# A message-passing kernel: grid of 36 slots instead of 32, five PSUM banks for its groups, and the block's maximum in PSUM

## What is computed

```python
z = x @ enc_node_w + enc_node_b           # of relu(layernorm(x))
e = edge_attr @ enc_edge_w + enc_edge_b
def genconv(z, e, src, dst, w1, b1, g1, bb1, w2, b2, t):
    msg = relu(z[src] + e) + 1e-7
    m = msg * t
    ex = exp(m - segment_max(m, dst)[dst])
    agg = segment_sum(msg * ex, dst) / segment_sum(ex, dst)
    out = z + agg
    return relu(layernorm(out @ w1 + b1) * g1 + bb1) @ w2 + b2
# layer 0: h = genconv(z, ...); layers 1..3: h += genconv(relu(layernorm(h)), ...)
# result: x + relu(layernorm(h))
```

## Time and profile before

| | us |
|---|---|
| median of 3 runs (6206.5 to 6214.1) | 6207.28 |
| the profiled execution, its own time | 6218.0 |
| its span, first to last instruction | 6213.7 |
| `prepare`, 0 to 509 | 509 |
| `lay`, 509 to 1759.5 | 1250.5 |
| layers 0, 1, 2 (to 2860, 3965, 5071) | 1100.5, 1105, 1106 |
| the last layer, 5071 to 6213.7 | 1142.7 |

### The profile page before, as it was taken

How to read it: one execution, slowest core, us unless ns; L and a number is a source line. 1 busy time by engine, 2 the same in 40 slices (tenths; PEclk the granted TensorE clock), 3 DMA queues, 4 the chain that set the end, 5 groups by cost and what they waited for, 6 DMA issues and landing times. The chain is left out here.

```text
span 6213.7 us, 106997 instructions
## 1 busy us (share of the span) xinstructions
PE 4575.7 (74%) x43556; PEld 3238.2 (52%) x43557; DVE 4593.2 (74%) x7210; ACT 2450.6 (39%) x3848; POOL 4185.6 (67%) x3850
## 2 busy tenths in 40 slices
PE   7715888999938777783777877468777756777786
PEld 6715777888825444452445544244544533454443
DVE  9431555444438999994899999489999957888887
ACT  2403566654513444441444443234434423333333
POOL 3054777766547777774777777377777747777775
PEclk8955888666669998896899889789988978898888
DMA  8971777665564555544455555445555534454552
GB/s 344 417 239 66 260 275 282 221 234 221 194 192 167 180 174 185 177 164 118 157 178 183 175 176 177 126 144 179 170 183 177 184 130 136 165 173 165 169 173 88
DMA packets 323285, 1168.13 MB, mean 188 GB/s; under 512 B 142130, under 2 KB 145380, under 8 KB 255444
## 3 DMA queue, kind: packets, MB, share of 16 engines
q1 hardware_dynamic: 172852, 890.91, 38.7%
q0 software_dynamic: 134800, 214.63, 13.7%
q10 hardware_dynamic: 15120, 55.50, 2.2%
HBM read 910.82 MB, written 249.92 MB: 187 GB/s over the span
## 5 line engine op out<-in xcount | busy, mean ns | idle before, releaser
L1258 POOL DMA_INDIRECT gb<-ztab,ovi x2704 | 2945.6, 1089 | 1025.3 <-issue 833.6
L1356 PE MATMUL bank<-ep_mid,keep 128*128 128x512 f32 (+3 forms) x3474 | 1568.1, 610 | 18.8 <-DVE ep_mid L1346 18.8
L1356 PEld LDWEIGHTS bank<-ep_mid,keep 128*128 128x128 f32 x3474 | 699.3, 203 | 853.1 <-issue 820.7
L1309 DVE TENSOR_REDUCE mx<-xb 128x64 f32<-128x2816 f32 (+17 forms) x196 | 1016.7, 5187 | 3.6
L1273 PE MATMUL bank<-zpw,oh_layers 128*128 128x64 bf16 x28812 | 879.7, 194 | 155.9 <-DMA zpw<-ztab 155.9
L1273 PEld LDWEIGHTS bank<-zpw,oh_layers 128*128 128x128 bf16 x28812 | 874.3, 98 | 211.1 <-DMA zpw<-ztab 156.9
L1096 POOL DMA_INDIRECT ecell<-zpw,ptg x588 | 646.8, 1100 | 228.1 <-issue 176.7
L1404 PE MATMUL bank<-keep,na 128*128 128x128 f32 x100 | 47.5, 475 | 952.8 <-DVE na L1401 952.8
L925 PE MATMUL bank<-byk,zpw 88*88 88x102 f32 (+13 forms) x4608 | 665.1, 332 | 53.0 <-DVE zpw L906 49.1
L925 PEld LDWEIGHTS bank<-byk,zpw 88*88 88x88 f32 (+13 forms) x4608 | 654.5, 234 | 62.8 <-DVE zpw L906 54.0
L1319 ACT ACTIVATE cm<-top_x,nt 128x64 f32<-128x64 f32 x196 | 68.2, 348 | 1501.4 <-DVE top_x L1313 1484.9
(11 more groups left out here) (222 smaller groups left out, 5784.6 us busy)
## 6 DMA issues: line engine op xcount, KB each, us to landing
oh_layers<-ohd SPq DMA_DIRECT2D x196, 1568.0 KB, 9.8
ea_in<-in_ea SPq DMA_DIRECT2D x101, 512.0 KB, 8.1
enc<-es_out ACTq DMA_DIRECT2D x101, 512.0 KB
cb<-rowc SPq DMA_DIRECT2D x49, 1024.0 KB
gb<-ztab,ovi POOLq DMA_INDIRECT x2704
ohd<-oh_lay SPq DMA_DIRECT2D x49, 576.0 KB
xb<-ecell SPq DMA_DIRECT2D x20, 1408.0 KB
ohd<-oh_lay SPq DMA_DIRECT2D x49, 512.0 KB
```

What stands on the lines that cost most here:

```text
L1258: at["g"][d] = ga_l[d % 2](GP.indirect_dma_start(gb[d % 2][:, 64 * v:64 * v + 64], None, T["ztab"], bass.IndirectOffsetOnAxis(ap=ovi[:, i: ...
L1309: q = V(VE.tensor_reduce(mx[:, 0:64], x_of(d, 0, S.S[d]).rearrange("p (s f) -> p f s", f=64), AX.X, ALU.max))
L1356: q = PE.matmul(both[d % 2][:, 0:w], ident, rows[:, 128 * (c - a):128 * (c - a) + w], start=(c == 0), stop=(c + 4 >= S.S[d]), skip_group_c ...
```

## The change

G becomes 36, with 23 groups of one source block and 13 of two. `OVER` becomes 36, 21, 20, ... 5, 628 in all, so that V is 5, 36, 6, 21, 6, 20, 7, ... 12 and the slots are 49*36 + 628 = 2392. A block's grid has five groups of eight (the last of four), each with its bank: `gps` is banks 0 to 4. `both` is one bank, 5; `NA` and `NB` are the halves of bank 6; `top_x` is 128 columns of bank 7. ScalarE makes `cm` from `mx`, now two tiles by turns, with a Relu of its own ahead of the exponential. The two bias products move behind TensorE's wait for ScalarE. The sums of block d wait for the fold of block d-1. In `lay`, `pick` takes 6 slots at a time in place of 20.

```diff
-OVER = (39, 23, 21, 20, 19, 19, 18, 18, 17, 17, 17, 16, 16, 16, 16, 15, 15, 15, 15, 14, 14, 14, 14,
+OVER = (36, 21, 20, 19, 18, 18, 17, 17, 16, 16, 16, 15, 15, 15, 15, 14, 14, 14, 14, 13, 13, 13, 13,
...
-        self.singles = 15
+        self.singles = 23
...
-            hit = sb("hit", [128, 20 * KS], FP32, yc)
+            hit = sb("hit", [128, 6 * KS], FP32, yc)
-                for a in range(0, S.S[d], 20):
-                    n = min(20, S.S[d] - a)
+                for a in range(0, S.S[d], 6):
+                    n = min(6, S.S[d] - a)
-                share = 1.1 * (len(eights) * (len(units[u]) + put) + 4 * put + 1) / steps
+                share = 1.1 * (len(eights) * (len(units[u]) + put) + 9 * put + 1) / steps
...
-                n_gp = 4
+                n_gp = 5
-                gps = bank[0:4]
-                both, NA, NB = bank[4:6], bank[6], bank[7]
+                gps = bank[0:5]
+                both, NA, NB = bank[5], bank[6][:, 0:256], bank[6][:, 256:512]
+                top_x = bank[7][:, 0:128].rearrange("p (a f) -> p a f", a=2)
...
+                    top = mx[:, 64 * (d % 2):64 * (d % 2) + 64]
-                    q = V(VE.tensor_reduce(mx[:, 0:64], x_of(d, 0, S.S[d]).rearrange(
+                    q = V(VE.tensor_reduce(top, x_of(d, 0, S.S[d]).rearrange(
-                    q = k["topx"][d] = V(VE.tensor_scalar(top_x[:, d % 2, :], mx[:, 0:64], 0.0,
+                    q = k["topx"][d] = V(VE.tensor_scalar(top_x[:, d % 2, :], top, 0.0,
-                    q = A(AE.activation(cm[:, u % 2, i, :], top_x[:, d % 2, :], ACT.Exp,
+                    q = A(AE.activation(cm[:, u % 2, i, :], top, ACT.Relu))
+                    AE.wait_ge(ae_s, q)
+                    q = A(AE.activation(cm[:, u % 2, i, :], cm[:, u % 2, i, :], ACT.Exp,
...
-                    if i == 0 and d >= 2:
-                        PE.wait_ge(ve_s, k["fold"][d - 2])
+                    if i == 0 and d:
+                        PE.wait_ge(ve_s, k["fold"][d - 1])
...
                     q = A(AE.copy(ot[:, :], NB[:, 0:128]))
-                    PE.matmul(NA[:, 0:256], ident, b1, start=True, stop=False)
                     yield
                     PE.wait_ge(ae_s, q)
+                    PE.matmul(NA[:, 0:256], ident, b1, start=True, stop=False)
                     q = P(PE.matmul(NA[:, 0:256], ot[:, :], w1, start=False, stop=True))
...
-                    PE.matmul(NA[:, 0:128], ident, b2, start=True, stop=False,
-                              skip_group_check=True)
                     yield "turned"
...
                     PE.wait_ge(ae_s, q)
+                    PE.matmul(NA[:, 0:128], ident, b2, start=True, stop=False,
+                              skip_group_check=True)
```

More of the change, by code:

```diff
@@ L19 @@
 RSQRT_SEED = 0x5F3759DF
-OVER = (39, 23, 21, 20, 19, 19, 18, 18, 17, 17, 17, 16, 16, 16, 16, 15, 15, 15, 15, 14, 14, 14, 14,
-        13, 13, 13, 13, 12, 12, 12, 12, 12, 11, 11, 11, 11, 10, 10, 10, 10, 9, 9, 9, 9, 8, 8, 7, 7, 6)
+OVER = (36, 21, 20, 19, 18, 18, 17, 17, 16, 16, 16, 15, 15, 15, 15, 14, 14, 14, 14, 13, 13, 13, 13,
+        12, 12, 12, 12, 12, 11, 11, 11, 11, 11, 10, 10, 10, 10, 9, 9, 9, 9, 8, 8, 8, 7, 7, 6, 6, 5)
 EDGES = (64,) + (54,) * 2 + (52,) * 2 + (50,) * 4 + (48,) * 8 + (46,) * 8 + (44,) * 10 + (42,) * 14
@@ L57, in __init__ @@
         self.ones = [sum(n for _, n in self.groups[:s]) for s in range(self.G + 1)]
-        assert self.ones[-1] == self.ND and self.G == 32
+        assert self.ones[-1] == self.ND and self.G == 36
         self.sorted = [d // 2 if d % 2 else self.ND - 1 - d // 2 for d in range(self.ND)]
@@ L93 @@
 for _n, _w in (("ident", 128), ("iota", 128), ("be", 128), ("prow", 2),
-               ("base", 32), ("full", 49), ("iota1", 128), ("we", 128), ("wn", 128), ("bn", 128), ("cen", 128),
+               ("base", 36), ("full", 49), ("iota1", 128), ("we", 128), ("wn", 128), ("bn", 128), ("cen", 128),
                ("ms", 2), ("lower", 128), ("shift", 128), ("wrap", 128), ("node", 49),
@@ L720, in sorted_path @@
                 mx = sb("mx", [128, 64 * -(-S.SP // 2)], FP32, fc)
-                top_x = sb("top_x", [128, 2, 64], FP32, fc)
                 cm = sb("cm", [128, 2, 2, 64], FP32, fc)
@@ L727, in sorted_path @@
                 oh2 = sb("oh_layers", [128, 2, 128 * S.ones[-1]], BF16, fc)
-                layer_args = (oh2, z, h, npd, wri, dci, outi, ovi, xb, gb, mx, top_x, cm, ds, nt,
+                layer_args = (oh2, z, h, npd, wri, dci, outi, ovi, xb, gb, mx, cm, ds, nt,
                               zb, zr)
@@ L1200, in layer @@
         def layer(number, tag, args):
-            (oh, z, h, npd, wri, dci, outi, ovi, xb, gb, mx, top_x, cm, ds, nt, zb, zr) = args
+            (oh, z, h, npd, wri, dci, outi, ovi, xb, gb, mx, cm, ds, nt, zb, zr) = args
             final = tag == "last"
@@ L1355, in mul @@
                         w = 128 * min(4, b - c)
-                        q = PE.matmul(both[d % 2][:, 0:w], ident, rows[:, 128 * (c - a):128 * (c - a) + w],
+                        q = PE.matmul(both[:, 0:w], ident, rows[:, 128 * (c - a):128 * (c - a) + w],
                                       start=(c == 0), stop=(c + 4 >= S.S[d]),
@@ L1366, in fold @@
                     k["fold"][d] = V(VE.tensor_reduce(
-                        ds[:, u % 2, i, :], both[d % 2][:, :].rearrange("p (g c) -> p c g", g=4),
+                        ds[:, u % 2, i, :], both[:, :].rearrange("p (g c) -> p c g", g=4),
                         AX.X, ALU.add))
```

## The result

The changed kernel takes 6311.68 us (median of 4 runs, 6284.73 to 6323.16), the kernel before 6210.69 on the same chip (median of 4 runs, 6206.5 to 6214.76): ratio 1.0156, 95% interval 1.0122 to 1.019. That is 101 us slower; forecast was 6350. The profiled execution took 6307.63 us, its span is 6303.2.

The account below looks back on a forecast made before the run. VectorE was taken to pace the three middle layers, GpSimd the last. Middle layers +59 each (+177), last layer -27, layout -8: total +142 us, so 6218.0 becomes 6360 profiled, median about 6350; range 6285 to 6405.

Parts of the forecast that it names:

- VectorE's added work: Per layer: more reduction, sub, mul and a fifth add, less over; together 57.4 us, about 52 with overlap, taken as 55.
- waits ahead of the splitting: Middle layers: VectorE's waits for ScalarE's casts shrink by 9 us, and by 3 more from shorter first slices.
- wait for `hb`: Every layer: only the fifth add covers this step, so VectorE waits 0.55 us 25 times, +14 us.
- L1432, now L1435: Node chain: later bias products and longer sums use up TensorE's slack, so this wait grows by 6 us a layer.
- start: Start of each layer: the first two blocks have 41 gathers in place of 45, -5 us.
- last node stage: End of each layer: the last node stage adds 1 us.
- crowded first pairs: Last layer: nearly all of 103 us of gather waits goes, but 5 us is kept for these pairs.
- (1): Splitting in middle layers: the 1.62 us wait stays for the second cast, only 0.36 goes; -9 us, and -3 from shorter exponentials.
- (2): Step waiting for `hb`: no longer covered by over, VectorE waits 0.55 us there, +14 us in every layer.
- shorter rounds of `pick`: Layout: a round no longer holds TensorE up, about 1 us for each of two rounds in seven units, -15 us.
- The rival of the wider units: Layout: four units widened to 96 to 100 columns leave the low clock, each 9 us shorter, total 6315; 25%, inside the range.
- `turn_back`: Layout: its copies grow with the slots by 6%, some 0.8 us in each of nine units, +7 us.

Follow-up runs that it names:

- experiment 7: Changed kernel with separate banks for NA and NB, bias products ahead of TensorE's wait, and the maximum in SBUF: 6264.86 us.
- experiment 6: Changed kernel without the two node-stage steps that follow the fifth add, so the old order of steps: 6283.53 us.
- experiment 2: Changed kernel with the maximum back in SBUF, everything else as changed: 6309.61 us.
- experiment 1: Kernel before with only the maximum moved to PSUM, and one bank for the sums to make room: 6167.36 us, ratio 0.9941.
- experiment 3: Changed kernel with one more node-stage step ahead of the first sub, for earlier casts: 6185.14 us.

## Why the prediction was right, and where its sizes were off

The side, the mechanism and the place were right, and the time lay in the range; the sum was 52 us too high, 23 of them in the middle layers, 20 in the last and 9 ahead of layer 0. Point by point, for the third layer:

| term of the sum | forecast | measured |
|---|---|---|
| VectorE's added work | +55 | +49.7 |
| waits ahead of the splitting | -12 | -10.9 (49.7 to 38.8) |
| wait for `hb` | +14 | +11.6 (1.7 to 13.3) |
| L1432, now L1435 | +6 | +4.9 (10.3 to 15.2) |
| start | -5 | -5.0 (36.1 to 31.1) |
| last node stage; measured at the layer's last fold | +1 | +2.4 (L1366, now L1369, 10.9 to 13.3) |
| sum | +59 | +52.7; the stretch grew by 51.2 |

Two of the waits before, which the rows ahead of the prediction don't have:

```profile
DVE ds L1366 <- PE bank L1356: 10.9, 2, 9.2
...
DVE na L1439 <- ACT hb L263: 1.7, 2, 0.8
```

**VectorE's added work** is the term that was mis-sized most. Its instructions add up to 55.7 us more (the sums by line: the fifth `add` 20.3, the reduction 16.5, `sub` 10.7, `mul` 11.8, `over` -3.3, the others together -0.3), near the 57.4 of the sum; but the engine is busy only 49.7 us longer (940.3 to 990.0), since 6.0 us lie under their neighbours. The prediction had measured this overlap, worked 52 out of it, and then took 55 without a reason. That is 5 of the 8 us by which each middle layer was over-estimated, some 16 us of the 52. The wait for `hb` gives 2 more: the sum took all of it for new.

**What each part cost.** Of the 51.2 us of the third layer, 10.3 go with the banks and the bias products undone (experiment 7), 3.3 with the moved steps (experiment 6), none with the maximum's place (experiment 2). The other 38 are left for the wider grid itself, by subtraction: no run has it alone.

**The last layer** lost 42.4 us, not 22. Its waits for gathers fell by 109.3 us (136.9 to 27.6): all but the start, so that the 5 us kept for crowded first pairs was too much. VectorE's work grew by 53.0, its wait for `hb` by 11.6 (1.7 to 13.3), and L1435 did not grow at all (13.8 to 13.4). That TensorE's longer chain shows in a middle layer and not in this one, I can't explain.

**GpSimd.** The prediction held that the gathers beside `sub` make no difference to the sum, because VectorE has no room; experiment 2 shows it for the changed kernel. It holds only there: in the kernel before the same relief is worth 41 us (experiment 1), all in the last layer. Of the gathers that start while L1332 runs, 306 of 389 take more than 1.05 us in the trace of before, in the mean 0.54 us more than one alone, and beside L1346 313 of 373; in the changed kernel none of 531 beside L1335 (the longest takes 0.95 us), and 321 of 348 beside L1349. The Trainium skill, page SBUF — State Buffer, section "Who interferes with whom", says that a VectorE instruction with two SBUF inputs contends with a GpSimd instruction that reads SBUF, and that one with at most one SBUF input, outside the 2-port perf modes, doesn't; the traces agree with both halves of it.

**The maximum's place.** The sum gave PSUM no price, and `sub` shows none: 1484 ns against 1483 for `mul`, and in experiment 2, with the maximum in SBUF, the 121 `sub`s of a layer take 178.3 us against 177.6. The prediction's estimate from the Trainium skill, page VectorE: DVE Perf Modes, section on the TRN2 errata, was 31 us; the measurement decides against it here.

**Casts.** (1) and (2) of the prediction came out as worked out: 1.62 us stays ahead of the second splitting, 0.50 us (0.55 forecast) stands ahead of L1442. Experiment 3 shows the cause: with the second cast ahead of the exponential the 38.8 us of waits go, and 38 to 43 us with them in every middle layer.

**TensorE.** The term was right in size by offsetting errors. The wait at L1435 grew by 4.9 us for the forecast 6, but undoing the change of banks and bias products takes 10.3 us from this layer, and leaves a wait of 8.9, under the 10.3 of before. So the effect of the moved products and the shared bank was under-estimated, and the rest of the term, which is the longer sums, was over-estimated: with them alone the wait is no longer than before.

**Layout.** From the first `spread` to the last it took 1168 us before and 1151 after, -17 for the forecast -8. That this is near is luck: the -15 us for shorter rounds of `pick` didn't come, and the gain is the rival's, from units that left the low clock. TensorE's waits for the one-hot matrices in the last nine units, before and after:

```profile
PE bank L925 <- DVE zpw L906: 15.4, 6, 4.1
```

```profile
PE bank L924 <- DVE zpw L905: 14.2, 13, 8.3
```

In the timeline before, two of the six waits, 3.6 us in all, stand behind a round of `pick`; the other four, 11.8 us, behind a comparison (L1004) that itself came late. After, eleven waits of 0.3 to 0.4 us, 4.3 in all, stand behind `pick`, and the longest, 8.3 us in unit 13, behind a comparison that waited for its DMA:

```profile
1376.15 0.48 DVE L1003 TENSOR_SCALAR oh_lay<-cb,keep 128x1024 bf16<-128x1024 bf16 x1 [11.62 <-DMA cb<-rowc]
```

The rival of the wider units came true by half. Units 9 (92x100) and 10 (92x98) of the changed kernel:

```profile
1103.70:1132.90 29.20, 26.85 (x259) 25.55 (x258) 25.14 (x60) 13.18 (x30) 20.76 (x19) 0.92 0.88 324
1160.90:1205.10 44.20, 44.20 (x260) 44.11 (x261) 28.34 (x67) 13.10 (x30) 34.45 (x33) 0.50 0.68 262
```

Of the four units with 96 to 100 columns two had left the low clock in this execution (9 and 12), three in experiments 2, 3, 6 and 7. Each that does takes 55 to 59 us from start to start in place of some 70, which is 11 to 16 us less, not 9. In this execution the two gave 30 us; the first nine units took 6 us more than before, and the other seven of the last nine together 6 more. Units 11 and 16, at 0.50 and without a wait in both traces, are 0.9 and 0.5 us longer, near the 0.8 forecast for `turn_back`. The spread of the changed kernel's runs, 38 us where before has 8, would follow from units that leave the low clock in one execution and not in another; that is argued, since only the profiled execution has a trace. The other 5 us ahead of layer 0 lie in `prepare`, which is the same in both kernels; the first `spread` starts between 538 and 550 us in all kernels on these chips.

**Medians.** The forecast took the profiled execution's +142 over to the median. The span grew by 89.5 us, the median by 101: the profiled execution of the kernel before was 7 us above its median of 6210.69, that of the changed kernel 4 under its own.

## What to carry to other kernels

Where two engines are both near full, find for each stretch by its waits which one is later and by how much the other is behind: taking 48 us of waits a layer off VectorE here gave 17, until GpSimd, whose margin that was, had been relieved too; the two edits together gave twice the sum of what each gave alone. Work may be moved only onto the engine that waits; this grid moved 48 gathers a layer off an engine that had a margin in three of four layers, onto one that had none. A wait that is set by another engine's instruction order can be cheap to remove: here one more step in the interleaving took 126 us from the changed kernel. And a sum that comes out near the measured time is no proof of its terms: two of them, the layout's and TensorE's, were near by errors that offset each other.

## What the runs showed of the hardware

- An indirect DMA of GpSimd takes 0.94 to 0.95 us alone and up to 2.5 beside a VectorE instruction that reads two operands from SBUF; with one of them in PSUM the delay is gone, and VectorE takes the same time either way.
- TensorE in the layout has two lasting conditions: products of 92x94 f32 one after the other without a gap at a granted clock of 0.50 (1.2 GHz), 44 us for a unit, or 29 to 36 us at 0.74 to 0.93. The size bears on it: in the last nine units of these traces those of 88 rows were always in the first, those of 92 rows mostly (those of 96 to 100 columns now so, now so), those of 96 rows never. It doesn't settle it: one earlier unit of 96x102 was in the first, for 45 us (experiment 3). Four to eight more rows of zeros in nine units made the kernel 80 us faster.
- Another chip of this kind ran the same kernel in 8074 us instead of 6207; in a variant of it, traced there, TensorE stood still for 1448 us ahead of one group of products. A comparison is only worth something beside the kernel before on the same chip.
